# A Macaron layer pair on one core: the soft mixture's turned operands made by DMA transposes instead of TensorE transposes

## The reference

```python
x = x + 0.5 * _L0_ffn_ref(_layernorm(x), ...)   # 4-bit quantised gated MLP, inner size 704 ("f0")
x = x + _L0_attn_ref(_layernorm(x), ...)        # retention with decay ("a0")
x = x + 0.5 * _L0_ffn_ref(_layernorm(x), ...)   # "f0" again
x = x + 0.5 * _L1_ffn_ref(_layernorm(x), ...)   # soft mixture of 8 experts x 128 slots ("f1")
x = x + _L1_attn_ref(_layernorm(x), ...)        # causal attention, 16 heads, low-rank terms ("a1")
x = x + 0.5 * _L1_ffn_ref(_layernorm(x), ...)   # "f1" again
```

```python
xn = rms_norm(x, gamma_x); se = rms_norm(slot_embeds, gamma_slot)
logits = einsum('bsd,etd->bset', xn, se)            # 512 tokens x 1024 slots
dispatch = softmax(logits, axis=1)                  # over the tokens
slots = einsum('bsd,bset->betd', xn, dispatch)
h = gelu(slots @ w1); processed = h @ w2
combine = softmax(logits over all 1024 slots)       # over the slots
out = einsum('bnd,bsn->bsd', processed, combine)
```

## Time and profile before

| | before |
|---|---|
| median of 3 runs | 2572.69 us (2568.84 to 2573.86) |
| profiled execution | 2571.66 us, of which the span on the core is 2569.9 us |
| mean granted TensorE clock | 0.965 of full speed |
| f1 steps | first normalised rows at 528.3 us, last combine matmuls at 2565 us |

### The profile page before, as it was taken

One profiled execution on the slowest core, in us unless ns is written; L12 is line 12 of the kernel. 1 busy time (PEld: TensorE's weight loads), 2 busy tenths in 40 slices (PEclk: granted clock), 3 DMA queues, 4 the chain that ended last, 5 costly groups with the idle time before them and its releaser, 6 DMA issues.

```text
span 2569.9 us, 54204 instructions
## 1 busy us (share of the span) xinstructions
PE 2314.0 (90%) x22616; PEld 1777.8 (69%) x22616; DVE 1878.7 (73%) x3184; ACT 1668.6 (65%) x2917; POOL 885.6 (34%) x631
## 2 busy tenths in 40 slices
PE   2889889889989898999899899999989898899999
PEld 2566566657777776767687677677667676687788
DVE  8689889998787967777777686868776776552631
ACT  4377666647676674776766767476575748685666
POOL 0122222222413322462534535353463526332122
PEclk7899999999999999999999999999999999999999
DMA  5000000000000000000000000000000000000000
GB/s 177 19 1 1 1 1 1 1 1 1 1 1 1 1 1 26 2 26 2 14 14 2 26 2 16 12 14 14 23 14 10 16 20 2 10 2 9 9 10 9
DMA packets 34979, 33.05 MB, mean 13 GB/s; under 512 B 7664, under 2 KB 34096, under 8 KB 34736
## 3 DMA queue, kind: packets, MB, share of 16 engines
q1 hardware_dynamic: 34736, 29.60, 3.5%
HBM read 12.54 MB, written 4.19 MB: 7 GB/s over the span
## 4 chain that ended last, share of the span: by engine, by line
PE 66%; DVE 20%; ACT 5%; issue 4%; POOL 2%; SPq 2%; DMA 1%; DVEq 0%; ACTq 0%
PE psum L749 17%; PE psum L751 16%; PE psum L750 15%; PE psum L755 6%; PE psum L1186 2%; PE psum L1037 2%; PE psum L1188 2%; PE psum L1187 2%; PE psum L1090 2%; PE psum L1067 2%; SPq L724 1%; POOL a1pr L2181 1%; DVE a1pr L1943 1%; DVE f0hT L1810 1%; PE psum L1017 1%
## 5 line engine op out<-in xcount | busy, mean ns | idle before, releaser
L2194 POOL TENSOR_TENSOR f1hT<-f1g,f1hT 128x512 f16<-128x512 f32 x256 | 308.9, 1211 | 655.1 <-ACT f1hT L1596 654.4
L2181 POOL TENSOR_TENSOR a1pr<-a1PT,a1pr 128x1024 f16<-128x1024 f32 (+1 forms) x176 | 357.5, 2033 | 302.9 <-DVE a1pr L1943 302.8
L749 PE MATMUL psum<-f1w2h,f1hT 128*128 128x256 f16 x1024 | 282.9, 276 | 8.8 <-issue 7.3
L749 PE MATMUL psum<-f1sl,f1w1h 128*128 128x256 f16 x1024 | 282.2, 276 | 9.5 <-ACT f1g L1591 7.6
L751 PE MATMUL psum<-f1w2h,f1hT 128*128 128x256 f16 x1024 | 282.2, 276 | 0.0
L750 PE MATMUL psum<-f1w2l,f1hT 128*128 128x256 f16 x1024 | 282.1, 275 | 0.0
L750 PE MATMUL psum<-f1sl,f1w1h 128*128 128x256 f16 x1024 | 281.2, 275 | 0.0
L751 PE MATMUL psum<-f1sl,f1w1l 128*128 128x256 f16 x1024 | 281.0, 274 | 0.0
L1920 DVE TENSOR_REDUCE a1nm<-psum 128x2 f32<-128x768 f32 (+3 forms) x176 | 198.1, 1126 | 84.8 <-PE psum L1017 83.9
L1943 DVE CAST a1pr<-a1PT 128x1024 f16<-128x1024 f32 (+1 forms) x176 | 167.9, 957 | 80.6 <-ACT a1PT L1493 58.2
L2170 POOL TENSOR_TENSOR f0h<-f0Y,f0sc 128x704 f32<-128x704 f32 x64 | 93.2, 1457 | 342.3 <-DVE f0Y L1798 342.3
(11 more groups left out here) (339 smaller groups left out, 6835.2 us busy)
## 6 DMA issues: line engine op xcount, KB each, us to landing
a1Q<-a1st SPq DMA_DIRECT2D x96, 64.0 KB, 2.6
a1K<-a1st SPq DMA_DIRECT2D x96, 64.0 KB, 2.6
x<-in_L_attn_x SPq DMA_DIRECT2D x8, 512.0 KB, 7.8
out<-x SPq DMA_DIRECT2D x8, 512.0 KB, 3.0
wslot<-in_L_ffn_w SPq DMA_DIRECT2D x1, 1024.0 KB, 9.5
wraw<-in_L_ffn_w SPq DMA_DIRECT2D x1, 1024.0 KB, 5.6
wslot<-in_L_ffn_slot_embeds SPq DMA_DIRECT2D x1, 1024.0 KB, 7.9
a1Q<-a1mr SPq DMA_DIRECT2D x64, 4.0 KB, 1.7
```

Source lines behind the costliest of these rows:

```text
L749: e.matmul(out, lh, rh, start=start, stop=False)
L2181: e.tensor_tensor(a1["pr"][:, i % 2, 1, :, 0:w], a1["PT"][:, i % 2, :, 0:w], a1["pr"][:, i % 2, 0, :, 0:w], ALU.subtract).then_inc(s["a1_pl"])
L2194: e.tensor_tensor(hT1[:, c % 2, 1, 2 * hp:2 * hp + 2, :], gg[:, hp % 2, :, :], hT1[:, c % 2, 0, 2 * hp:2 * hp + 2, :], ALU.subtract).then_ ...
```

## The change

For the f1 steps alone, the turned operands no longer pass through PE and PSUM. The rows are split first (`xn_h` by ACT, `xn_l` by DVE, as before), and SP then issues five DMA transposes for each step: four of 128x256 float16 from `xn_h` and one of 128x1024 from `xn_l`, into a rearranged `f1xT`. The exponentials are split in SBUF: ACT copies `u[:, hf]` as float16 into `ub`, DVE subtracts into the other half of `ub`, and SP issues one DMA transpose of 128x1024 (both pieces of the 512 columns) into `eT`, eight in each step. `ub` lies in the memory of `xn`. So ACT's first copy waits for `xn_l` (`f1_nl`) and for the DMA before it of the same half (`f1_t0`, `f1_t1`), and the next step's normalised rows wait until all eight DMAs of this step have landed. The logits wait for all five row transposes (`f1_x`), the combine for `f1_t0` and `f1_t1`. The third pair of f1 banks goes. The planner's cost for issuing a DMA goes from 60 to 635 ns, and a DMA transpose gets 1290 ns. Due times near these pieces shift by a few microseconds, and three semaphores of the weights' preparation are merged into one.

```diff
+    def dma_start_transpose(self, out, src):
+        return self.note(1290, None, 2.0 * out.shape[0] * self.each(out))
+
     def dma_start(self, out, src, **kw):
-        return self.note(60, None, out.shape[0] * self.each(out) * (2 if out.dtype == mybir.dt.float16 else 4))
+        return self.note(635, None, out.shape[0] * self.each(out) * (2 if out.dtype == mybir.dt.float16 else 4))
...
+        ub = xn[:, :, :].rearrange("p t d -> p (t d)").bitcast(f16).rearrange("p (i m n) -> p i m n", i=2, m=2)
...
+            def f1_rows(j):
+                S = at_f1(j)
+                yield S + 8.0
+                q.wait_ge("f1_nh", j + 1)
+                q.wait_ge("f1_lg", 8 * j)
+                for t in range(NT):
+                    e.dma_start_transpose(f1xT[:, 0, t, :, :], xn_h[:, t, 0:D]).then_inc(s["f1_x"], 16)
+                yield S + 10.0
+                q.wait_ge("f1_nl", j + 1)
+                e.dma_start_transpose(f1xT[:, 1, :, :, :].rearrange("p t k n -> p (t k) n"), xn_l[:, :, :].rearrange("p t d -> p (t d)")).then_inc(s["f1_x"], 16)
+
+            def f1_second(j):
+                S = at_f1(j)
+                for n in range(8):
+                    t, hf = divmod(n, 2)
+                    yield S + f1_e2_at(n) + 2.4
+                    q.wait_ge("f1_ul", 8 * j + n + 1)
+                    q.wait_ge("f1_cb", 2 * j)
+                    e.dma_start_transpose(eT[:, hf, :, :, qrows(t)].rearrange("p m i s -> p (m i) s"),
+                                          ub[:, hf, :, :].rearrange("p m n -> p (m n)")).then_inc(s[f"f1_t{hf}"], 16)
...
             def f1_front(j):
                 S = at_f1(j)
-                for k in range(2):
-                    yield S + 6.5 + 0.8 * k
-                    q.wait_ge("f1_u", 4 * j + 4)
-                    bk = 4 + k
-                    v = bank(bk)
-                    for t in range(NT):
-                        ins = tr(v[:, t * P:(t + 1) * P], xn[:, t, k * P:(k + 1) * P])
-                    ins.then_inc(s["f1_xT"])
-                    banks.after(bk, "f1_xl", 2 * j + k + 1)
                 for n in range(8):
...
+                    q.wait_ge("f1_x", 80 * (j + 1))
...
-            def f1_second(j):
-                S = at_f1(j)
-                for n in range(8):
-                    yield S + f1_e2_at(n) + 1.3
-                    q.wait_ge("f1_ex", 8 * j + n + 1)
-                    q.wait_ge("f1_cb", 2 * j)
-                    bk = f1_banks(j)[2][n % 2]
-                    v = bank(bk)
-                    for i in range(4):
-                        ins = tr(v[:, i * P:(i + 1) * P], u[:, n % 2, i * P:(i + 1) * P])
-                    ins.then_inc(s["f1_eT"])
-                    banks.after(bk, "f1_Tl", 8 * j + n + 1)
...
-                    q.wait_ge("f1_eT", 8 * j + n - 1)
+                    q.wait_ge("f1_ul", 8 * j + n - 1)
...
-                    e.activation(eT[:, 0, 4 * hf:4 * hf + 4, qrows(t)], psum[:, f1_banks(j)[2][n % 2], :].rearrange("p (i s) -> p i s", i=4),
-                                 ACT.Copy).then_inc(s["f1_Th"])
+                    yield S + f1_e2_at(n) + 0.9
+                    q.wait_ge("f1_ex", 8 * j + n + 1)
+                    q.wait_ge("f1_nl", j + 1)
+                    q.wait_ge(f"f1_t{hf}", 16 * (4 * j + t))
+                    e.activation(ub[:, hf, 0, :], u[:, hf, :], ACT.Copy).then_inc(s["f1_uh"])
...
-                q.wait_ge("f1_xT", 2 * j)
                 q.wait_ge("f1_nh", j)
                 q.wait_ge("f1_nl", j)
+                q.wait_ge("f1_t0", 64 * j)
+                q.wait_ge("f1_t1", 64 * j)
...
-                    e.tensor_tensor(eT[:, 1, js, qrows(t)], psum[:, f1_banks(j)[2][n % 2], :].rearrange("p (i s) -> p i s", i=4), eT[:, 0, js, qrows(t)],
-                                    ALU.subtract).then_inc(s["f1_Tl"])
+                    yield S + f1_e2_at(n) + 1.6
+                    q.wait_ge("f1_uh", 8 * j + n + 1)
+                    e.tensor_tensor(ub[:, hf, 1, :], u[:, hf, :], ub[:, hf, 0, :], ALU.subtract).then_inc(s["f1_ul"])
```

More of the change, by code:

```diff
@@ L101, in f1_banks @@
 def f1_banks(j):
-    return ((4, 5), (4, 5), (4, 5)) if j < B + LATE else ((4, 5), (0, 1), (2, 3))
+    return ((4, 5), (4, 5)) if j < B + LATE else ((4, 5), (0, 1))
 A0_GROUPS = (((0,), 4, P), ((1,), 5, P), ((3, 2), 6, 0))
@@ L596, in build @@
         xn_h, xn_l = sb("f1xnh", [P, NT, D + 2], f16, stD), sb("f1xnl", [P, NT, D], f16, stD)
-        f1xT = sb("f1xT", [P, 2, 2, T], f16, stD)
+        f1xT = sb("f1xT", [P, 2, NT, 2, P], f16, stD)
         e1 = sb("f1e", [P, 2, 2, NT, 2 * P], f16, stD)
-        eT = sb("f1eT", [P, 2, 8, T], f16, stD)
+        eT = sb("f1eT", [P, 2, 2, 4, T], f16, stD)
         u = sb("f1u", [P, 2, 512], f32, stD)
         xn = sb("f1xn", [P, NT, D], f32, stD)
+        ub = xn[:, :, :].rearrange("p t d -> p (t d)").bitcast(f16).rearrange("p (i m n) -> p i m n", i=2, m=2)
         dd = sb("f1d", [P, NS], f32, stD)
@@ L737, in last @@
                 q.wait_ge("out", 16 * B)
-            return [weights(), *[chain(z, B) for z in (load, a1_moves, store)], last()]
+            return [weights(), *[chain(z, B) for z in (load, a1_moves, store)],
+                    *[chain(z, 2 * B) for z in (f1_rows, f1_second)], last()]
         def tensor(e, q, banks):
@@ L816, in retention_weights @@
                         ins = tr(v[:, m * D + k * P:m * D + (k + 1) * P], raw0["v"][:, k * D + m * P:k * D + (m + 1) * P])
-                ins.then_inc(s["w_vT"])
-                banks.after(7, "w_vc", 1)
+                ins.then_inc(s["w_vo"])
+                banks.after(7, "w_vo", 2)
                 yield 47.5
-                q.wait_ge("w_vc", 1)
+                q.wait_ge("w_vo", 2)
                 v = bank(6)
@@ L1136, in f1_front @@
                     v = bank(bk)
+                    q.wait_ge("f1_x", 80 * (j + 1))
                     for k in range(2):
-                        q.wait_ge("f1_xl", 2 * j + k + 1)
-                        ins = three(v, f1xT[:, 0, k, qrows(t)], f1xT[:, 1, k, qrows(t)], se[0][:, k, ns], se[1][:, k, ns], k == 0, k == 1)
+                        ins = three(v, f1xT[:, 0, t, k, :], f1xT[:, 1, t, k, :], se[0][:, k, ns], se[1][:, k, ns], k == 0, k == 1)
                     ins.then_inc(s["f1_lg"])
@@ L1267, in f1_combine @@
                             q.wait_ge("f1_pl", 4 * j + k // 2 + 1)
-                            ins = three(v[:, i * D:(i + 1) * D], eT[:, 0, k, qs], eT[:, 1, k, qs], pr1[:, 0, k, :], pr1[:, 1, k, :], k == 0, k == 7)
+                            ins = three(v[:, i * D:(i + 1) * D], eT[:, k // 4, 0, k % 4, qs], eT[:, k // 4, 1, k % 4, qs], pr1[:, 0, k, :], pr1[:, 1, k, :], k == 0, k == 7)
                     ins.then_inc(s["f1_cb"])
@@ L1274, in tensor @@
                   *[chain(z, B) for z in (a0_front, a0_values, a0_scores, a0_out, a1_front, a1_first, a1_maxima, a1_second, a1_values, a1_out)],
-                  *[chain(z, 2 * B) for z in (f1_front, f1_slots, f1_slots2, f1_second, f1_mlp, f1_mlp2, f1_combine)]]
+                  *[chain(z, 2 * B) for z in (f1_front, f1_slots, f1_slots2, f1_mlp, f1_mlp2, f1_combine)]]
         def scalar(e, q, banks):
@@ L1330, in retention_weights @@
                 yield 46.5
-                q.wait_ge("w_vT", 1)
-                e.activation(wvT, psum[:, 7, :], ACT.Copy).then_inc(s["w_vc"])
+                q.wait_ge("w_vo", 1)
+                e.activation(wvT, psum[:, 7, :], ACT.Copy).then_inc(s["w_vo"])
             def straight():
@@ L1512, in f1_front @@
                 S = at_f1(j)
[L1513 to L1516, removed]
                 for n in range(8):
                     t, hf = divmod(n, 2)
-                    yield S + 11.5 + 2.3 * n
+                    yield S + 13.8 + 2.0 * n
                     q.wait_ge("f1_lg", 8 * j + n + 1)
@@ L2005, in f1_front @@
                     e.tensor_scalar(xn[:, t, :], xb[:, b, t, :], mv[:, t, 0:1], rstd[:, 2, t:t + 1], ALU.subtract, ALU.mult).then_inc(s["f1_u"])
[L2006 to L2009, removed]
                 for t in range(NT):
@@ L2038, in f1_rows @@
             def f1_rows(j):
-                yield at_f1(j) + 10.5
+                yield at_f1(j) + 7.6
                 q.wait_ge("f1_nh", j + 1)
```

17 lines of the change are left out of this document (6 added, 11 removed), and 4 rows, old and new, of the table s.

## The result

The changed kernel takes 2547.5 us (median of four runs, 2545.1 to 2550.7) against 2573.1 us for the kernel before, measured beside it: a ratio of 0.9905, 95% interval 0.9888 to 0.9922, so 25 us less. The direction was forecast; the size was 49 us less, and half of that came. The profiled execution has a span of 2548.6 us.

What follows compares the result with a forecast made beforehand. TensorE, 93% busy from 530 to 2570 us, was taken to bound the f1 part. The terms -54 - 8 + 10 + 3 = -49 us gave 2524 us, 1.9% less, with a range of 2486 to 2590 us.

Steps and rivals of the forecast that it cites:

- TensorE's time: f1 steps: 640 transposes leave TensorE, 70 us of work, taken as 54 us less by their share of the chain.
- Idle before the transposes: TensorE's 16.8 us of idle directly before the removed f1 transposes: half goes, 8 us less, bounds 0 and 17.
- The exponentials' way: Exponential to eT grows from 1.9 to 4.3 us, hidden in the expert part except once at the end: 3 us more.
- The rows' longer way: Normalised rows to operands: 6.5 us longer in each f1 step, a tenth exposed, 10 us more, bounds 0 and 104.
- The slower rival of the exposed front: Five serial DMAs before each f1 step's first logit are exposed: +56 us (2629) to +122 us (2695); chance 0.12.
- that of the slow DMA: f1 DMA transposes far longer than copies: fit up to 12 us each, at 15 us 370 us more (2940); chance 0.05.
- VectorE, ScalarE and SP at nothing: Splitting and issuing in f1 cost nothing: VectorE's change covered by idle, ScalarE 15 us less, SP under a third busy.
- The planner's order: New order of SP's queue, a1's Q and K moves behind DMA transposes: 0 us, either sign possible up to 19.1.
- The signs of being wrong: TensorE's f1 share under 88% with waits on f1xT, f1eT or a1Q; landing over 8 us; pre-530 us stretch moving over 5 us.

Runs made afterwards that it cites:

- e13: Kernel before in its own order, each group of four f1 transposes emitted as one 512-column matmul (35 us less TensorE work): 2555.1 us, ratio 0.9926.
- e14: Kernel before in exactly its own order, each of the 640 f1 transposes done twice (70 us more TensorE work): 2625.2 us, ratio 1.0197.
- e15: Changed kernel in exactly its own order, but ub in its own memory with two buffers for each half: 2518.2 us, ratio 0.9786.
- e7: Changed kernel with the same memory cut into one float32 u and a ring of three float16 pairs: 2544.7 us, ratio 0.9903.
- e4: Kernel before with only the planner's cost of a DMA issue raised from 60 to 635 ns: 2514.7 us, ratio 0.9788.
- e12: Changed kernel with GpSimd's lag in the planner moved from 100 to 101 ns: 2565.6 us, ratio 0.9975.

## Why the prediction was wrong

**TensorE's time, -54 us: mis-sized.** That 640 transposes go, at 0.11 us, was right: busy time fell 64 us in the f1 part. Their worth was read from the chain, 0.77 us for each us. At a fixed order it is 0.55 downward (e13), so -38 us if the second half of the 70 is like the first, which no run tests. A likely reason, which no run isolates: the chain is one path, and when it gets shorter the next path takes over. e14 fits this, since added work costs more, 0.73. Part of the shortfall, 8 us of busy time in e13, is the clock, below.

**Idle before the transposes, -8 us.** No run separates it. TensorE's waits for f1u are gone, and larger ones stand elsewhere.

**The exponentials' way, +3 us at the very end: this step failed.** I wrote that it "has the whole expert part to hide in". The data can wait that long, but ScalarE can't: the cast n waits for the DMA of cast n-2 and stands in order in front of Gelus and a1's exponentials. I had named the wait for the buffer in the description of the change and then priced only the latency to `eT`. The runs price it, together with the rows' wait for the shared memory: 31 us at the fixed order (e15). The length of the way alone doesn't give this: casts of one half are due 8 us apart in the kernel, and the bare way, cast, subtraction and landing, is 4.2 us in the trace, near my 4.3. What I left out is that the DMA of cast n-2 can start late: SP holds the first ones of a step until the combine of the step before has freed `eT` (20 of the 45 us of waiting), and VectorE's subtraction is often late behind other work (18 us). The bare way accounts for 3 us. The ring of three (e7), which tightens `u` in exchange, gained nothing in its order.

**The rows' longer way, +10 us.** The way was right (issue 1.25 to 1.31, landing 2.4 and 2.8 us), the exposed part smaller: TensorE waited 4.6 us in all for f1xT, and rows alone by DMA add no idle time in the table. The slower rival of the exposed front did not happen, nor did that of the slow DMA: 2.8 us is far from its 12.

**VectorE, ScalarE and SP at nothing.** VectorE's subtractions took 111.6 us (forecast 119), the casts 629 ns (629). SP issued in 1.23 us (1.29). These held.

**The planner's order, 0 us with "both signs, up to 19".** This bound was far too small, and it is the larger failure. Four orders of the structure before lie between 2515 and 2572 us, four of the changed one between 2533 and 2574. The kernel before is the slowest of its four. Put together at the fixed-order prices, the change is worth about -38 + 31 = -7 us, an estimate; 25 were measured, and the other 18 lie well inside the spread of the draws. They were not traced to a place. So that the time fell clearly at all, as forecast, is for the most part luck of the order. From the table the changed structure is even 0.0044 (11 us) slower in the mean, with a standard error of about 15 us (standard deviations 0.0087 and 0.0078, four orders each). So whether the change as a structure is faster or slower than the one before stays open. That it becomes faster with a second buffer in memory of its own is shown at one fixed order by 31 us; the two pairs of changed and two-buffer kernels under the same planner (plain and nudged) agree.

**The signs of being wrong** that the prediction had named did not show: TensorE's share in the f1 part is 90.6%, landing is far under 8 us, and the first normalised rows start at 531.6 us after 528.3. All three looked at TensorE and the DMA, and none at ScalarE, where the loss arose.

**The landing.** The Trainium skill, page "Advanced Engine Details and Errata", section "X-Bar Transpose (TRN2)", has transposing DMAs as fast as plain ones. The trace agrees: in the changed kernel the transposes of 128x256 float16, 64 KB each, land in 2.4 us and plain copies of 64 KB in 2.6; 256 KB transposed take 2.8 us.

```profile
a1Q<-a1st SPq DMA_DIRECT2D x96, 64.0 KB, 2.6
...
f1xT<-f1xnh SPq DMA_TRANSPOSE x64, 2.4
```

The issue on SP is twice that of a copy, 1.23 us against 0.59.

## What to carry to other kernels

When an operand moves to a path with a longer latency, count the buffers first, against that latency and against all that can hold the transfer back (here the single `eT`): a producer that must wait for its buffer holds up its whole engine, not only its own data. A share of the chain was too high a price for what is taken away: it said 0.77 for each us, and at a fixed order 0.55 came. And where an order comes from a search over a cost model, measure how far a meaningless nudge moves the time (here 15 to 50 us in six nudges, 0.6 to 1.9%) before a gain of that size is believed, and compare causes at a fixed order.

## What was not expected of the hardware

At a fixed order the granted clock of TensorE moved with its work, against the change. The runs of e13 (work taken away) had a mean granted clock of 0.959 to 0.961, those of the kernel before beside them 0.959 to 0.966, and those of e14 (work added) 0.967 to 0.970; the ranges of the first two overlap. The clock has two levels, 1.2 and 2.4 GHz. In the profiled executions TensorE was at the lower one for 130 us of the f1 part in e13, 108 in the kernel before and 90 in e14. Half of such a difference is work lost or won, about 11 and 9 us, which fits what is missing in both: busy time fell by 27 us where 35 us of work were taken, and rose by 62 where 70 were added.

Between orders the clock moves as much with no work changed: e4's runs have 0.971 to 0.973 where the kernel before has 0.961 to 0.966, and e12's 0.945 to 0.951 where the changed kernel has 0.952 to 0.958. e4's 56 us are in part this: in the f1 part it is at the lower level for 72 us instead of 108, TensorE is busy 24 us less with the same instructions, and idle 33 us less. So the changed kernel's 0.956 against 0.965 can't be put down to the work that went. About half of its extra time at the lower level (93 us against 71) even lies before 530 us, where no transpose was removed.

The page "VectorE: DVE Perf Modes" of the Trainium skill, section "The three transpose paths", gives 1309 ns for one 128x128 transpose by DMA; here the DMA of eight such blocks landed in 2.8 us. For SP the size made hardly a difference: 128x256 took 1247 ns to issue and 128x1024 1234 (exponentials) or 1307 (rows).
